# Moving three input loads behind the first key copies, and two kinds of products into the list scheduler

## The reference

```python
# block 0 (block 1 is alike with silu(c), rotary positions and the tanh gelu)
ada = (c @ W_ada + b_ada)[:, None, :]
shift1, scale1, gate1, shift2, scale2, gate2 = jnp.split(ada, 6, axis=-1)
h = _layernorm(x) * (1.0 + scale1) + shift1
Q, K, V = h @ Wq + bq, h @ Wk + bk, h @ Wv + bv          # 16 heads of 8
attn = softmax(Q K^T / sqrt(8));  attn_out = (attn V) @ Wo + bo
x = x + gate1 * attn_out
h = _layernorm(x) * (1.0 + scale2) + shift2
return x + gate2 * (gelu(h @ W1 + b1) @ W2 + b2)
```

## Time and profile before

| | us |
|---|---|
| time of the runs, median of 3 (lowest, highest) | 417.49 (415.98, 418.70) |
| profiled execution: span from first to last instruction | 415.7 |
| TensorE busy in it | 388.4 (93%) |
| VectorE busy | 329.4 (79%) |
| ScalarE busy | 323.8 (78%) |
| POOL busy | 187.5 (45%) |

### The profile page before, as it was taken

How to read it: one execution, slowest core, us unless ns; L and a number is a source line. 1 busy time by engine, 2 the same in 40 slices (tenths; PEclk the granted TensorE clock), 3 DMA queues, 4 the chain that set the end, 5 groups by cost and what they waited for, 6 DMA issues and landing times. The chain is left out here.

```text
span 415.7 us, 10244 instructions
## 1 busy us (share of the span) xinstructions
PE 388.4 (93%) x3666; PEld 205.8 (49%) x3670; DVE 329.4 (79%) x768; ACT 323.8 (78%) x634; POOL 187.5 (45%) x290
## 2 busy tenths in 40 slices
PE   8699899999999999999999998999999999998996
PEld 3444343455544544554545544545555444435874
DVE  6497999989886499898899874899898889935343
ACT  5207786799898968887989887769797999895664
POOL 4539999525745155453162354171451320004564
PEclk9759999999999999999999998999999999999999
DMA  7700237210005000013000023000050000000001
GB/s 254 184 15 14 78 113 203 72 32 2 2 2 149 7 6 2 2 53 103 3 6 2 2 56 98 6 2 2 2 135 20 3 2 16 2 0 3 2 0 39
DMA packets 17186, 17.63 MB, mean 42 GB/s; under 512 B 2460, under 2 KB 15454, under 8 KB 17120
## 3 DMA queue, kind: packets, MB, share of 16 engines
q1 hardware_dynamic: 15840, 16.19, 13.8%
q10 hardware_dynamic: 1296, 0.79, 0.8%
HBM read 6.62 MB, written 0.52 MB: 17 GB/s over the span
## 5 line engine op out<-in xcount | busy, mean ns | idle before, releaser
L1397 DVE TENSOR_REDUCE mx<-max_ps 128x1 f32<-128x512 f32 x384 | 241.9, 682 | 30.3 <-PE max_ps L908 29.2
L1223 ACT ACTIVATE probs<-exp_ps 128x512 f32<-128x512 f32 x384 | 202.6, 605 | 29.4 <-PE exp_ps L917 28.3
L908 PE MATMUL max_ps<-k_stack,q_stack 64*128 64x512 bf16 x384 | 113.5, 390 | 6.9 <-DMA k_stack<-parts 3.5
L1098 PE MATMUL pv_ps<-probs,v_ones 128*32 128x256 f32 x1536 | 103.0, 385 | 4.5 <-ACT probs L1223 3.8
L917 PE MATMUL exp_ps<-q_stack,k_stack 64*128 64x256 bf16 x768 | 101.3, 271 | 0.6 <-ACT probs L1223 0.5
L1417 POOL TENSOR_SCALAR var_eps<-mv 128x2 f32<-128x2 f32 (+2 forms) x33 | 6.5, 198 | 131.1 <-DVE mv L1257 130.0
L1098 PEld LDWEIGHTS pv_ps<-probs,v_ones 128*32 128x32 f32 x1536 | 41.1, 109 | 42.7 <-ACT probs L1223 17.2
L908 PEld LDWEIGHTS max_ps<-k_stack,q_stack 64*128 64x128 bf16 x384 | 29.4, 93 | 61.9 <-DVE mx L1397 36.2
L917 PEld LDWEIGHTS exp_ps<-q_stack,k_stack 64*128 64x128 bf16 x768 | 43.3, 94 | 29.4 <-ACT probs L1223 11.5
L1235 ACT ACTIVATE mrows<-exp_ps 8x256 bf16<-8x256 bf16 x48 | 17.5, 365 | 17.5 <-PE exp_ps L1083 17.1
L1030 PE MATMUL exp_ps<-hT,w 128*128 128x256 f32 x96 | 29.3, 425 | 0.8 <-ACT hT L1157 0.8
(11 more groups left out here) (128 smaller groups left out, 485.1 us busy)
## 6 DMA issues: line engine op xcount, KB each, us to landing
k_stack<-parts SPq DMA_DIRECT2D x36, 128.0 KB, 2.5
q_stack<-parts SPq DMA_DIRECT2D x30, 128.0 KB
w<-in_w_dram SPq DMA_DIRECT2D x4, 448.0 KB, 3.3
w<-in_w_dram SPq DMA_DIRECT2D x4, 256.0 KB, 2.9
w<-in_ada_dram SPq DMA_DIRECT2D x1, 896.0 KB, 5.2
w<-in_rows_dram SPq DMA_DIRECT2D x1, 832.0 KB, 7.4
q_stack<-mrows SPq DMA_DIRECT2D x48, 4.0 KB
x<-in_x_dram SPq DMA_DIRECT2D x2, 256.0 KB, 3.5
```

The source lines that it names most:

```text
L908: return pe.matmul(max_bank(n), half(q_stack, b, pair, j)[:, t * P:(t + 1) * P], half(k_stack, b, pair, j), start=True, stop=True)
L1098: mm = pe.matmul(pv_ps[32 * j:32 * j + 32, cols_of(g // 2)], v_ones[:, b, kt, 4 * g + j, :], probs[:, (4 * i + j) % RING_P, cols_of(of_two ...
L1223: act.activation(probs[:, tile % RING_P, :], exp_bank(e), ACT.Exp, scale=SCORE_SCALE[hc // 2 // NB]).then_inc(exp_read, 1)
L1397: dve.tensor_reduce(mx[:, G % 2, t, 2 * (pair % 2) + j:2 * (pair % 2) + j + 1], max_bank(n), AX_X, ALU.max, negate=True).then_inc(max_read, 1)
```

## The change

The three loads (`ada` parts 2 to 15, parts 16 to 19, and `rows`) leave the head of the SP program and are issued behind DK 0's last part, so behind the six copies of the first keys and ahead of POS. ADA1 and all three GATE leave the fixed start and form a stream of the scheduler. ADA1 is ready once MAX 3 is done, a GATE once ADA1 is. The numbering of the banks starts accordingly.

```diff
@@ -63,7 +63,6 @@
 CLOCK_PRODUCTS = {"WO": 8, "W2": 6, "W2S": 6}
 FIRST_PRODUCTS = [16, 2, 4]
 SECOND_BATCH = 5.0
-EARLY_GATES = 1
 EARLY_ANGLES = 2
 WARM_BEATS = 10
 GATE_AFTER = 3
@@ -251,8 +250,10 @@
             return need(("cosine", name[1], k, h), *([("DQ", k - 1, WHOLE, 2)] if h == 0 else [("split", name if name == "RK" else "SQ", k, 0)] if name == "RK" else []))
         if name == "SQ":
             return need(("RQ", k, h, 0) if k >= NB else ("Q", k, h, 0), *([("DQ", k - 1, WHOLE, 2)] if k > 0 else []))
+        if name == "ADA1":
+            return need(("MAX", 0, GATE_AFTER))
         if name == "GATE":
-            return need(("MAX", 0, GATE_AFTER))
+            return need(("ADA1", 0, WHOLE, 0))
         if name == "XG0" and ("GATE", 0, WHOLE, 2) not in at:
             return None
         if name == "ANG":
@@ -388,11 +389,11 @@
     first = first[:2] + [("ADA0", 0, WHOLE, 0)] + first[2:]
     for item in first:
         order.append(item)
-    order.extend([("ADA1", 0, WHOLE, 0)] + [("GATE", 0, WHOLE, c) for c in range(EARLY_GATES)] + [("POS", 0, WHOLE, 0)])
-    streams.append([("GATE", 0, WHOLE, c) for c in range(EARLY_GATES, 3)])
+    order.append(("POS", 0, WHOLE, 0))
+    streams.append([("ADA1", 0, WHOLE, 0)] + [("GATE", 0, WHOLE, c) for c in range(3)])
     at.update({("DQ", 0, WHOLE, 2): 0.0, ("V", 0, WHOLE, 0): -3.0, ("split", "RK", 0, WHOLE): -3.0, ("split", "SQ", 0, WHOLE): -3.0,
                ("POS", 0, WHOLE, 0): 10.0})
-    max_no[0] = 2 + EARLY_GATES
+    max_no[0] = 1
     streams.append(with_counts(["ST", "XH", "TR", "K", "Q", "SQ"], 1, WHOLE))
     streams.append([("WARM", n, 0, 0) for n in range(WARM_BEATS)])
     streams.append([("V", 1, WHOLE, 0)])
@@ -786,9 +787,6 @@
             for j in range(HALVES):
                 sp.dma_start(vec_qk[64 * j:64 * j + 64, :], ins["vec"][j::HALVES]).then_inc(small_in, 16)
             sp.dma_start(x[:, 1], ins["x"][1].rearrange("(t p) d -> p t d", p=P)).then_inc(x_in[1], 16)
-            sp.dma_start(w[2][:, 0:14 * D], ins["ada"][:, 2 * D:16 * D]).then_inc(ada1_in, 16)
-            sp.dma_start(w[3][:, 0:4 * D], ins["ada"][:, 16 * D:20 * D]).then_inc(ada1_in, 16)
-            sp.dma_start(rows, ins["rows"].to_broadcast([P, 13 * D])).then_inc(rows_in, 16)
 
             def stack(k, which, part, target, of_part, split_done, split_no, done):
 
@@ -801,6 +799,12 @@
             def load_weights(n, cols):
 
                 sp.dma_start(w[n][:, cols], ins[f"w{n}"][:, cols]).then_inc(w_in[n], 16)
+
+            def load_modulation():
+
+                sp.dma_start(w[2][:, 0:14 * D], ins["ada"][:, 2 * D:16 * D]).then_inc(ada1_in, 16)
+                sp.dma_start(w[3][:, 0:4 * D], ins["ada"][:, 16 * D:20 * D]).then_inc(ada1_in, 16)
+                sp.dma_start(rows, ins["rows"].to_broadcast([P, 13 * D])).then_inc(rows_in, 16)
 
             def background(G):
 
@@ -841,6 +845,8 @@
                         sp.wait_ge(ones_tile_set, 1)
                         sp.dma_start(k_stack[MAX_SLOTS, k], ones_rows[:, :].unsqueeze(1).to_broadcast([4, PAIRS, S])).then_inc(ones_set[k], 16)
                     stack(k, 0, c, k_stack, PARTS_K, split_k, SPLIT_K_NO, stacked_k)
+                    if k == 0 and c == 2:
+                        load_modulation()
                 if name == "DQ":
                     if c == 0 and k == 1:
                         sp.wait_ge(q_zero[k], 1)
```

## The result

| | runs | median us | ratio to before |
|---|---|---|---|
| before | 4 | 418.10 | |
| after | 4 | 427.80 (427.53 to 429.79) | 1.0244 [1.0200, 1.0287] |

The brackets hold a 95% interval. The change makes the kernel 2.4% slower. The forecast was 423.0 with a range up to 427.0: the sign is right, the time is above the range. The profiled execution has a span of 425.8 us, 10.1 more than before; that difference is what the rest explains, where the forecast had 5.5.

A forecast was written before the change was run, and what follows sets the result against it. Bound: VectorE's MAX reductions from 54 to 84 us, then TensorE to 130, so a late start isn't hidden. Terms 2.5 + 1.9 + 1.1 = 5.5 on 417.49 gave 423.0 us; range 412 to 427.

The forecast's parts named there:

- (a): Loads issued behind six key copies, at about 16.2 us: gain 0, ADA1 not delayed, bound +2.
- (b): ADA1 behind the tenth MAX, where two gates stood: 5.2 us at 1.2 GHz against 3.75, +1.5.
- (c): Up to ROWS, one MAX and four WARM beats between: ROWS at 33.3, +2.5 with (b) inside, bounds +1.4 and +3.5.
- (d): ROWS to first EXP, with gates, transposes and an angle product between: 5.7 us against 3.84, +1.9; EXP at 39.0.
- (e): MAX: next one at about 39.3, +5.5 us, carried to the end because VectorE and TensorE are full.
- rival 3: Newly decided list closes the gaps before 139 and 260.46 us: faster, 411.3 us; chance 0.15.
- The term of 1.1: Part of the +5.5 at the next MAX: MAX falls 1.1 us further behind than EXP.
- (f): POOL: RED ahead of the gate biases, folded weights some 9 us later, covered before the first projection: 0, bound +2.
- Rival 1: Clock back at 30 us as before, so +3.3, 420.8 us; chance 0.20.
- Rival 2: VectorE's gap between 130 and 139 us swallows 4 of the 5.5: 419 us; chance 0.14.
- Rival 4: Further waits: 1.2 GHz up to EXP (+3), or load, fold or positions late (+2 each): 426 to 429; chance 0.13.

The follow-up runs named there:

- e1: Changed kernel and list, but the three loads back at the head of SP's program: 428.61 us, 1.0241 to before.
- e3: Loads late, changed list up to the first EXP, old order from there: 424.77 us, 1.0162 to before.
- e12: Changed list up to the 184th MAX, what is left in the old order: 425.36 us, 1.0192 to before.
- e13: Old list and start, loads at the head, up to the 184th MAX, then the changed order: 421.30 us, 1.0084 to before.
- e9: e6 plus one product of 512 columns behind each of the first twelve MAX: 422.96 us, 1.0142 to before.
- e14: e9 plus one product of 512 columns behind each of ADA1's products but the last: 421.26 us, 1.0100 to before.
- e16: Kernel before plus 15 wide products ahead of the first MAX, one behind each of ten MAX, two behind each angle product: 416.91 us, 0.9993.
- e2: Kernel before, list unchanged, with the three loads moved behind the first key copies: 426.84 us, 1.0198 to before.
- e6: e3 plus 29 products of 512 columns behind V of chain 0, before the first MAX: 423.79 us, 1.0147 to before.
- e17: ADA1 and all gates in fixed start, old order; wide products: six behind last GATE, one per first ten MAX, two per angle product: 419.80 us.

## Why the prediction was wrong

**(a) The loads: held.** Nothing on the path to the first MAX or to ADA1 waits for them, and e1 shows that their place is worth nothing. The sentence with the Trainium skill, "DMA: Bandwidth & Descriptors", section on queues, rings and completion order, had the first MAX up to 1 us later by turn-taking between queue rows; the trace doesn't show it, the first MAX came at 19.42 against 19.59. The last of the first query copies is issued by 15.4, one microsecond ahead of the first load, and what the first MAX waits for is still a key copy; the query copies land within 3.5 us, as before.

**(b), (c) ADA1 and the WARM beats: right in kind, 0.8 short.** ADA1 5.2 us at 25.06, ROWS at 34.10 for 33.3. I let the clock return within the beats, at 2.5 us; it returned at their end, 3.38. It is inside the bound of +3.5.

**(d) ROWS to EXP: 0.7 short.** 34.10 to 40.48 is 6.4 for 5.7: I had left out one projection of chain 1 (1.0) and two MAX (0.3) which the list puts ahead of the last gate, and priced the gates 0.4 high.

**(e) Carried to the end: the step that failed.** I carried 5.5 us to the end on the ground that VectorE and TensorE are full behind the start. That much holds: with the old order behind the new start the lag stays at 6.6 us to the last reduction (e3). What failed is that I took the rest of the list as unchanged while the start shifts. The scheduler had decided it anew, and its order costs by itself, behind the 184th MAX: 3.0 us behind the new start (e3, e12) and 3.6 behind the old one (e13), at like clock. The start at 6.7 us (e3) instead of 5.5, and this order at 3.0 to 3.6 instead of nothing, make 9.7 to 10.3; measured are 10.1. I had followed the scheduler's steps up to the first EXP only, and let a re-decided list appear only as a rival on the fast side (rival 3, closing the gaps before 139 and 260 us). It widened them, from 4.09 to 6.50 us and from 5.19 to 6.32.

The term of 1.1 within (e) didn't come either. It had 12 MAX issued by the first EXP and the next one at 39.3; there are 14, and the 13th is at 38.06, 4.4 us late where EXP is 5.9 late. So that the start's sum of 5.5 lies near these 5.9 is in part luck: (c) and (d) were 1.5 short, and this term 1.1 too high.

**(f) POOL: held.** RED ran ahead of the gate biases, the folded weights came at 83.80 for "near 84", the projection didn't wait for them.

**Rivals.** Rival 1 (clock back at 30) fell: it stayed at 0.50 up to 33.8. Rival 2 (shift absorbed before 139 us) fell: with the old order 6.6 us stand before and behind the gap. Rival 4 has the measured time in its range of 426 to 429, with the wrong terms. On the clock, can't tell what ADA1's products do to it: TensorE is busy 0.05 of 3.00 us in the stretch that reads 0.55. The runs e9 and e14 tell more: behind the narrow products it fell although the engine never paused, and with wide ones between them it held. In e16 it fell within ADA1, at 14.9, again without a pause ahead. The Trainium skill, "TensorE: Matmul & The Clock Gate", Part 1, says that sustained matmul activity releases the throttle; by that rule e9 should have kept its clock, and its trace doesn't agree. What stays open is why the second stretch comes at 255 us in one kernel and in the tail in another, though the instructions of the tail are the same.

## What to carry to other kernels

When a change touches a list scheduler's inputs, the whole list is new: compare the two orders to the end before carrying a shift, and splice them (new head, old rest) to price the parts. Independent small products belong under a wait that exists anyway; ADA1 in the wait for the keys cost nothing, and behind the tenth MAX 4.5 to 6 us. Late loads cost nothing here with a late first user (e1), and 9.2 us with an early one (e2).

## What the hardware showed

- 24 matmuls of two columns, busy without a pause at full clock, were followed by a fall to half clock (e9, at 29.4 us); with eleven products of 512 columns among them it didn't come in three of four executions (e14; the fourth had a mean clock of 0.984), and 11 added products made the median 1.7 us shorter.
- Products that fill a wait ahead of the MAX stage moved the fall from 16.6 to 23.6 us (e3, e6) and gained at most 1 us (424.77 to 423.79). With one more product behind each of twelve MAX it was 422.96 (e9), and only with wide products in ADA1 too 421.26 (e14).
- The same instructions at the same distance from each other got half clock in one kernel and full clock in another (the tail at 380.97 before and at 389.05 after; 1.67 us for the seven that the trace has, and 3.47 for eight). Executions of one kernel scatter by up to 6 us with the mean clock: those of e17 go from 414.85 at a mean clock of 1.000 to 420.69 at 0.980.
